# A mixed attention and expert kernel: normalisations by one two-scalar VectorE pass, the weight spreading on 128 rows, and the order set anew

## The reference

```python
def _layernorm(x, axis=-1, eps=1e-05):
    m = jnp.mean(x, axis=axis, keepdims=True)
    v = jnp.var(x, axis=axis, keepdims=True)
    return (x - m) / jnp.sqrt(v + eps)
...
x = x + _L0_xattn_ref(_layernorm(x, axis=-1), ctx_1024, ctx_1024, ...)
x = x + _L0_ffn_ref(_layernorm(x, axis=-1), ...)
x = x + _L1_xattn_ref(_layernorm(x, axis=-1), ctx_1024, ...)
x = x + _L1_ffn_ref(_layernorm(x, axis=-1), ...)
```

## Time and profile before

| | us |
|---|---|
| median of 3 runs | 326.61 |
| lowest, highest | 326.35, 327.21 |
| the profiled execution, its own time | 327.92 |
| its span in the trace | 325.9 |
| PE busy | 288.5 |
| DVE busy | 227.1 |
| ACT busy | 175.5 |
| POOL busy | 104.2 |

### The profile page before, as it was taken

How to read it: one execution, slowest core, us unless ns; L and a number is a source line. 1 busy time by engine, 2 the same in 40 slices (tenths; PEclk the granted TensorE clock), 3 DMA queues, 4 the chain that set the end, 5 groups by cost and what they waited for, 6 DMA issues and landing times.

```text
span 325.9 us, 7477 instructions
## 1 busy us (share of the span) xinstructions
PE 288.5 (89%) x2845; PEld 207.0 (64%) x2845; DVE 227.1 (70%) x641; ACT 175.5 (54%) x360; POOL 104.2 (32%) x109
## 2 busy tenths in 40 slices
PE   4598985887999978999999999776899999889994
PEld 4555663746566644565656676544666999569993
DVE  4769777898475389727478253879579996886533
ACT  3573743443478635483735867233963669535551
POOL 5930649393542011000001000112122666242631
PEclk9899998596999999999999999999999999999999
DMA  7700352423300000000000000000003120040121
GB/s 239 278 0 3 99 173 59 159 95 101 97 11 31 0 2 0 0 3 3 2 0 2 0 2 3 0 3 0 2 0 143 55 99 2 3 194 2 57 78 32
DMA packets 6634, 16.54 MB, mean 51 GB/s; under 512 B 708, under 2 KB 3016, under 8 KB 6600
## 3 DMA queue, kind: packets, MB, share of 16 engines
q1 hardware_dynamic: 6600, 16.08, 14.3%
HBM read 10.83 MB, written 0.52 MB: 35 GB/s over the span
## 4 chain that ended last, share of the span: by engine, by line
PE 65%; DVE 21%; POOL 5%; ACT 3%; issue 3%; DMA 1%; POOLq 0%; SPq 0%; DVEq 0%; ACTq 0%
PE ps L801 7%; PE ps L803 7%; PE ps L802 7%; PE ps L1037 6%; PE ps L984 4%; DVE MX L1405 3%; PE ps L955 3%; PE ps L953 3%; PE ps L956 2%; PE ps L874 2%; PE ps L862 2%; PE ps L1099 2%; PE ps L943 2%; PE ps L1129 2%; PE ps L863 2%
## 5 line engine op out<-in xcount | busy, mean ns | idle before, releaser
L1405 DVE TENSOR_REDUCE MX<-ps 128x8 f32<-128x512 f32 (+2 forms) x80 | 49.7, 680 | 13.4 <-PE ps L904 8.7
L1187 ACT ACTIVATE room<-ps 128x384 f32<-128x384 f32 (+1 forms) x96 | 46.2, 537 | 23.4 <-PE ps L956 15.3
L750 POOL TENSOR_SCALAR rstd<-mv 128x4 f32<-128x4 f32 x14 | 3.8, 272 | 134.1 <-DVE mv L1363 134.0
L773 POOL TENSOR_TENSOR wl<-wraw,wh 128x512 f16<-128x512 f32 (+1 forms) x30 | 35.6, 1215 | 31.7 <-DVE wh L1296 31.7
L664 POOL TENSOR_TENSOR room<-room 128x512 f16<-128x512 f32 x28 | 32.8, 1176 | 39.2 <-ACT room L1231 39.1
L812 PE MATMUL ps<-cst 128*128 128x128 f32 x142 | 25.0, 310 | 5.2 <-DMA cst<-in_const 4.2
L1037 PE MATMUL ps<-wd,room 128*128 128x128 f32 x144 | 23.3, 317 | 3.8 <-DVE room L1564 3.8
L812 PEld LDWEIGHTS ps<-cst 128*128 128x128 f32 x142 | 21.0, 216 | 8.2 <-DMA cst<-in_const 4.2
L1577 DVE TENSOR_TENSOR room<-ps,hr 128x512 f32<-128x512 f32 x28 | 19.1, 686 | 10.1 <-ACT hr L1225 8.8
L1037 PEld LDWEIGHTS ps<-wd,room 128*128 128x128 f32 x144 | 20.6, 222 | 6.5 <-DVE room L1564 4.4
L1231 ACT CAST room<-room 128x512 f16<-128x512 f32 x28 | 17.1, 618 | 11.7 <-DVE room L1577 11.5
(11 more groups left out here) (238 smaller groups left out, 836.7 us busy)
## 6 DMA issues: line engine op xcount, KB each, us to landing
wraw<-in_weights SPq DMA_DIRECT2D x8, 768.0 KB, 4.1
wraw<-wh SPq DMA_DIRECT2D x6, 384.0 KB, 2.9
wraw<-wl SPq DMA_DIRECT2D x6, 384.0 KB, 3.6
wraw<-in_weights SPq DMA_DIRECT2D x2, 576.0 KB, 7.3
rowb<-in_rows SPq DMA_DIRECT2D x1, 708.0 KB, 4.8
wd<-in_down SPq DMA_DIRECT2D x1, 576.0 KB, 7.4
X<-in_x SPq DMA_DIRECT2D x2, 256.0 KB, 4.4
picks<-in_spread SPq DMA_DIRECT2D x1, 512.0 KB, 5.7
```

The lines of the kernel that those rows point to most:

```text
L773: nc.gpsimd.tensor_tensor(wl[:, cols], wraw[:, i % 2, first:end], wh[:, cols], ALU.subtract).then_inc(w_ready, 1)
L1187: nc.scalar.activation(probabilities(a, b, u), src[:, 0:width], ACT.Exp, scale=SCALE[a]).then_inc(pr_ready, 1)
L1405: nc.vector.tensor_reduce(o, src[:].rearrange("p (h k) -> p h k", h=heads), AX_X, ALU.max).then_inc(max_read, 1)
```

## The change

- **Normalisations.** `ln_plain` is one piece on DVE: four `tensor_scalar` of 128 elements, one per token tile, (x - mean) * rstd with both as scalars per partition. DVE then waits for its own last one. `shift`, its semaphore and the ACT piece are gone.
- **Spreading.** `wpad` is 128 columns wide per tile instead of 64, so the transpose gives 128 rows; `wspread`, its copy and the matmul against `expsel` have 128 rows. The rows from 64 on are zero.
- **Rules.** In a pair of sequences the maxima of the second needn't come after the first's `negmax` any more; its `negmax` still does. The planner's cost of `ln_plain` is 1.0 on DVE.
- **Order.** `PRESSING` has other numbers, for 43 of the 49 entries of step.

```diff
-PRESSING = {..., 'ln_plain': 1411, 'ln_pow': 489, 'ln_stats': 1044, ...}
+PRESSING = {..., 'ln_plain': 1757, 'ln_pow': -1289, 'ln_stats': 1203, ...}
@@ attention()
-            before = [chain([("max", a, b, u) for u in range(12 if a == 1 else 4)] + [("negmax", a, b)], *before)]
+            before = [chain([("max", a, b, u) for u in range(12 if a == 1 else 4)], *before)]
+            chain([("negmax", a, b)], *before, *[("negmax", a, b - 1)] * (b % 2))
@@ parts()
     if k == "ln_plain":
-        return [("dve", .57), ("act", 1.65)]
+        return [("dve", 1.0)]
@@ build()
-        wpad = sb("wpad", [P, T, 64], F16)
+        wpad = sb("wpad", [P, T, P], F16)
...
-        wspread = [tF[0:64, g, 0:GT // 2].bitcast(F16) for g in range(G)]
+        wspread = [tF[:, g, 0:GT // 2].bitcast(F16) for g in range(G)]
...
-                        mm = nc.tensor.matmul(o[0:64, t * P:(t + 1) * P], wpad[:, t, :], identb[:], start=True, stop=True)
+                        mm = nc.tensor.matmul(o[:, t * P:(t + 1) * P], wpad[:, t, :], identb[:], start=True, stop=True)
...
-                        mm = nc.tensor.matmul(ps[bank[e][1]][:], expsel[0:64, x_:x_ + 1].broadcast_to([64, P]),
+                        mm = nc.tensor.matmul(ps[bank[e][1]][:], expsel[:, x_:x_ + 1].broadcast_to([P, P]),
                                               wspread[g], start=True, stop=True)
...
-                    nc.scalar.copy(wspread[e[1]], src[0:64, :]).then_inc(spread_ready, 1)
+                    nc.scalar.copy(wspread[e[1]], src[:]).then_inc(spread_ready, 1)
@@ ACT's queue
-                elif kind == "ln_plain":
-                    _, name, g = e
-                    from_, dst, _, _ = LN[name]
-                    k = nth[("ln_stats", name, g)] - 1
-                    sc.wait_ge(shift_ready, n)
-                    for t in range(T):
-                        ins = nc.scalar.activation(dst[:, g, t, :], from_[:, g, t, :], ACT.Identity, bias=shift[:, k, t:t + 1],
-                                                   scale=rstd[:, k, t:t + 1])
-                    ins.then_inc(plain_done, 1)
@@ DVE's queue
                 elif kind == "ln_plain":
-                    k = nth[("ln_stats",) + e[1:]] - 1
-                    dve.wait_ge(ln_rstd, nth[("ln_pow",) + e[1:]])
-                    for t in range(T):
-                        ins = nc.vector.tensor_scalar(shift[:, k, t:t + 1], mv[:, k, t, 0:1], rstd[:, k, t:t + 1], -1.0,
-                                                      ALU.mult, ALU.mult)
-                    ins.then_inc(shift_ready, 1)
+                    _, name, g = e
+                    from_, dst, _, _ = LN[name]
+                    k = nth[("ln_stats", name, g)] - 1
+                    dve.wait_ge(ln_rstd, nth[("ln_pow", name, g)])
+                    for t in range(T):
+                        ins = nc.vector.tensor_scalar(dst[:, g, t, :], from_[:, g, t, :], mv[:, k, t, 0:1], rstd[:, k, t:t + 1],
+                                                      ALU.subtract, ALU.mult)
+                    ins.then_inc(plain_done, 1)
+                    dve.wait_ge(plain_done, n)
```

More of the change, by code:

```diff
@@ L57 @@
 ARRIVES = {"ctx": 4.5, "masks0": 5., "masks1": 5., "bias": 7., ("split", 0): 5.5, "split": 14.0, ("ln_stats", "x0"): 7.0, "bo_add": 10.0, "kbs_zero": 8.5}
-PRESSING = {'add0': -408, 'add1': -1308, 'b3_add': -51, 'back': 744, 'bias': 929, 'bias_split': -399, 'bo_add': 1232, 'ctx': 951, 'down0': 576, 'down1': 359, 'downr': 1124, 'gate0': -1424, 'gate1': 1065, 'hi1': 1012, 'kblocks': -117, 'kbs_zero': -1339, 'ln_center': 83, 'ln_norm': 1593, 'ln_plain': 1411, 'ln_pow': 489, 'ln_stats': 1044, 'lo1': 1543, 'masks0': 320, 'masks1': 749, 'max': 334, 'nat': -86, 'negmax': 1829, 'o_take': -655, 'onehot': 426, 'onehot_t': -1823, 'out_norm': 1875, 'pv': -812, 'rank': 293, 'scores': -1610, 'sort_high': -1405, 'sort_low': 1667, 'spill': 245, 'split': 336, 'split_low': 436, 'spots': -1300, 'spread': 669, 'square': 1448, 'stack': -221, 'turn': 2557, 'up0': -841, 'up1': -41, 'v1': -1042, 'vctx': -868, 'xsplit': -353}
+PRESSING = {'add0': 63, 'add1': -1011, 'b3_add': 855, 'back': 391, 'bias': -267, 'bias_split': 1116, 'bo_add': 807, 'ctx': 1046, 'down0': -1303, 'down1': -1040, 'downr': 1177, 'gate0': -1424, 'gate1': 413, 'hi1': 1012, 'kblocks': -113, 'kbs_zero': -1339, 'ln_center': 367, 'ln_norm': 1835, 'ln_plain': 1757, 'ln_pow': -1289, 'ln_stats': 1203, 'lo1': -1154, 'masks0': -230, 'masks1': 760, 'max': 351, 'nat': -1025, 'negmax': 1917, 'o_take': -696, 'onehot': 936, 'onehot_t': -1823, 'out_norm': 1495, 'pv': -1096, 'rank': 818, 'scores': -1603, 'sort_high': -1404, 'sort_low': 1492, 'spill': 621, 'split': 336, 'split_low': 420, 'spots': -829, 'spread': 375, 'square': 871, 'stack': -221, 'turn': 2223, 'up0': 653, 'up1': -802, 'v1': -1399, 'vctx': -922, 'xsplit': -193}
 SHARED = 6
@@ L510, in build @@
         rstd = sb("rstd", [P, 7 * G, T])
-        shift = sb("shift", [P, 7 * G, T])
         lnx = sb("lnx", [P, G, T, P])
@@ L582, in build @@
         ln_stat, ln_rstd, ln_done = sem("ln_stat"), sem("ln_rstd"), sem("ln_done")
-        shift_ready, plain_done, b3_added = sem("shift_ready"), sem("plain_done"), sem("b3_added")
+        plain_done, b3_added = sem("plain_done"), sem("b3_added")
         centered = sem("centered")
```

## The result

The changed kernel took 336.99 us (median of 4 runs, 336.91 to 338.15) where the kernel before took 326.91 beside it: ratio 1.0329, 95% interval 1.0301 to 1.0357. The prediction was 324.3, with 330.5 as the top of its range. The profiled execution has a span of 335.0 us (325.9 before): PE busy 286.5 us (2.0 less), DVE 245.3 (18.2 more), ACT 164.0 (11.5 less), POOL 104.5 (as before). So PE was busy 2 us less and idle 11 us longer.

The account below looks back on a forecast made before the run. The prediction took PE to bound the kernel (65% of the last chain, DVE 21%). Its terms, 4.5 + 0.8 - 3.0 - 2.4 - 1.0 - 1.2 = -2.3, gave 324.3 us from a 326.61 median; 8-in-10 range 314 to 330.5.

Parts of the forecast that it names:

- The new order, "gives some 0.5 back": Start: both transposes first and attention 0's score maxima in a row were to return some 0.5 us.
- Start, +4.5: x0 at the start: group 1's pass held once per POOL addition or memset, delaying what follows; 4.5 us lost.
- x1 to the gates, +0.8: x1 to layer 0's gates: residues hold three of four passes per group, the second gate speeds up; net 0.8 us lost.
- The clock there, -3.0: Behind layer 0's second gate: PE stays busy, so the half-clock stretch goes; 3.0 us gained.
- Spreading, -2.4: Experts: with 128 rows, twelve spreading matmuls without a PE gap each save 0.2 us; 2.4 us gained.
- x2, -1.0: Handoff from layer 0, group 1: the unheld pass and steps covering PE's wait gain 1.0 us.
- x3 of group 0, -1.2: Third normalisation of group 0: PE waits there and POOL is free, so the shorter pass gains 1.2 us.
- x3 of group 1, 0: Third normalisation of group 1: 1.3 us saved, one or two holds paid; net 0, bounds -1 and +2.
- The third: Rival: all four instructions held at x0 group 1, x1 twice and x3 group 1; 329.5 us, chance 0.22.
- Rivals 1, 2 and 4: Memsets don't hold the pass: 318.9, chance 0.20; two-scalar form never held: 313.1, chance 0.13; spreading does nothing: 326.7, chance 0.05.

Follow-up runs that it names:

- e14: e7 with the order of the kernel before on PE, DVE and ACT up to the end of attention 0: 325.7 us.
- e7: e4 with x1 of both groups in the old form (shifts on DVE, normalisation on ACT): 328.4 us.
- e4: The changed kernel with POOL's two additions and its memsets made to wait for both passes of x0: 332.2 us.
- e2: The kernel before with the 128-row spreading alone, the shift written over the mean to make room: 324.9 us.
- e8: e2 with the pass on DVE only for x2 of both groups and x3 of group 0: 325.7 us.
- e11: e7 with attention 0's own steps on PE, DVE and ACT in the order of the kernel before, at the same queue places: 329.7 us.
- e13: The changed kernel with the order of the kernel before up to the end of attention 0, and x0 and x1 by shift and ACT: 323.9 us.
- e12: e11 with x3 of group 1 in the old form too (shift on DVE, normalisation on ACT): 329.1 us.
- e3: The changed kernel's order with the old normalisation (shifts on DVE, rest on ACT) and the 64-row spreading: 335.6 us.
- e15: The changed kernel with its order only from attention 0's end to mid attention 1, before's elsewhere; x0, x1 and x3 of group 1 by ACT: 322.5 us.
- e1: The kernel before, with its own order and 64-row spreading, and only the normalisation pass moved to DVE: 338.9 us.
- e10: e1 with POOL's additions and memsets made to wait for both passes of x0: 333.0 us.
- e6: The changed kernel with the same bytes zeroed by sixteen smaller memsets instead of three: 338.6 us.
- e9a: The changed kernel with POOL waiting for its own memset behind each of the two kbs memsets: 336.8 us.
- e9b: The changed kernel with a wait on an already satisfied semaphore in front of each of the three big memsets: 337.1 us.
- e5: The changed kernel with only POOL's memsets waiting for both passes of x0, the two additions left in place: 334.2 us.

## Why the prediction was wrong

The forecast was -2.3 us and the traces differ by +9.2 at the last product. Of the 11.5 between them, 5.8 stand in the start and attention 0 (+10.3 against +4.5), 4.4 between the second gate and layer 1's experts (-3.2 against -7.6), 2.0 in the last stage (+2.0 against 0), and x1 gives back 0.8 (0.0 against +0.8).

**The new order, "gives some 0.5 back": the step that failed most.** Attention 0 was priced in half a sentence inside the start's +4.5, from the fact that the maxima stand in a row. They do, and PE has too little beside them: +3.8 us from the first maximum to the end of attention 0, 1.9 with full clock and 1.9 from the half clock at 34 to 42 us. e14 gives 2.7 us for that order once nothing is held.

**Start, +4.5: right in kind, wrong in its rule and short by what follows.** It had each DVE instruction wait for one POOL instruction, "because the memsets use the same instruction stream as the additions". Additions and residues do that (1.17 to 1.24 us each). The second and third pass instead stayed until the row of memsets was over, so the pass ended at 19.9, not 17.7. That rule cost the forecast little: it had the bias split held by the last memset anyway, and `nat q0` came at 21.7, near its 21.0. What followed cost more than the 0.8 us allowed: with half clock to 24.7 us the first maximum came at +6.5, 1.7 more than `nat q0`.

**x1 to the gates, +0.8: right.** The holds are as drawn, three of four. From the end of group 0's attention 0 to the second gate's weights both kernels take 28.8 us: 2.85 lost ahead of the gate, 2.8 gained in it. The hold costs 3.8 us all the same (e7 against e4), because the faster gate doesn't need the held pass: e7 has it too.

**The clock there, -3.0: mostly not cashed.** The half clock behind the gate is gone in the changed kernel. Over 50 to 85 us before lost 8.5 us of full speed, the changed kernel in 60 to 95 only 3.4. But PE now rests instead (0.29 us of work in 84 to 86): half clock had stood where PE would have waited for DVE. From the gate to the first product of layer 1, where clock, spreading and both handoffs were to give 7.6 us, it gained 3.2. If the spreading gives its 2.2 here (e2) and the handoffs nothing (e8), some 1.0 is left for the clock; no run takes it by itself.

**Spreading, -2.4: right**, -2.2 in e2. **x2, -1.0, and x3 of group 0, -1.2: nothing came** (e8, in before's order). The wait of 1.69 us at the handoff is one of several that end together. **x3 of group 1, 0: +2.0 in the last stage**, at its upper bound. In the new order that stage took 82.3 us with the pass (changed, e7, e11, e13 and e14), and with the old form 81.7 in e12 but 82.7 in e3; in before's order 80.3 with the old form (e2, e8, e15) and 81.6 with the pass (e1, e10). So the order costs at least 1.4 there, and the pass 1.3 in before's order, held as at x1. What it costs in the new order isn't shown: e12 and e3 point opposite ways.

**Rivals.** The third, slower by full holds, had the right side with 329.5; its mechanism, all four instructions held, appears nowhere. Rivals 1, 2 and 4 are refuted by the 6.73 us, by x1 and by e2.

What isn't explained: why the clock falls in attention 0 in the changed kernel and e6, and not in e9a and e9b with the same order. The 2 us that e9a and e9b gain there are gone by the first product of layer 1: in both the clock is at half for some 3 us between 106 and 110.5, where the changed kernel has 1.00.

## What to carry to other kernels

Before work is moved to VectorE, ask what GpSimd does at that moment and what stands behind the instruction in VectorE's queue: one instruction of the pass took 0.34 us alone, 1.2 beside an addition, 6.7 beside an addition and a row of memsets. The queue behind it decided what that was worth: freeing the pass brought the first maximum 4.3 us forward in the new order (e4) and 6.4 in the old (e10). Saved latency at a wait is only worth what no other wait takes over; three places at 1.2 us gave nothing. And a new order should be tried in pieces: this one lost 2.7 us in front (by medians) and some 1.4 at the end, and gained 3.7 in the middle (by traces).

## What the runs showed of the hardware

- A row of GpSimd memsets can hold a VectorE `tensor_scalar` from SBUF to SBUF for longer than one of them: 6.73 us over the second addition and three memsets (6.62 in e1 and e9b), 7.27 over an addition and sixteen small ones, at most 2.93 with own waits between. It does not always: in e5 one was let in after the first of three memsets (1.98 us). What decides is not shown. The Trainium skill, "SBUF — State Buffer", section "Who interferes with whom", has the shared ports held for one whole instruction. The trace agrees for additions and residues (1.17 to 1.24 us) and for that instruction of e5, and not for the held passes.
- A `scalar_tensor_tensor` on 256 elements, all in SBUF, is held by an addition (1.37 us before, L1283) and not by a memset: 0.49 us in e5, from 17.07 on, inside a memset from 16.83 to 18.78.
- The two-scalar pass on f32 isn't faster than one with two tensors: 341 ns against 343, and 136 ns above the one-element shift's 205, about 1 ns per element. The Trainium skill, "VectorE: DVE Perf Modes", section "The perf-mode tier table", lists `tensor_scalar` on f32 at twice the plain speed; for this form, at 128 elements, no run here shows it. One-scalar forms that read f32 and write 16 bits took 0.22 us for 128 elements (L1266) and 0.35 for 256 (L1273); no run here tells whether the second scalar or the f32 output makes the difference.
- The norms with two tensors (L1386) are held too: four took 2.94 us at 269.96 beside POOL's residues of the hidden values, where one takes 0.34 us unheld (median). Maxima and products that read PSUM never were: all 80 maxima lie between 656 and 692 ns, and the 16 products of layer 0 between 673 and 690.
- A weight load of 64 rows isn't loaded ahead as one of 128 is. Before, the load of L1025 started at 84.78, 0.30 us after the matmul in front of it and with its own (84.79); now it starts with the matmul in front (90.34), 0.22 us ahead of its own. That was worth 2.2 us for 16 of them (e2). PE's loads, before and then now:

```profile
84.78 0.09 PEld L1025 LDWEIGHTS ps<-tF,expsel 64*128 64x128 bf16 x1 [0.42 <-issue]
```
```profile
90.34 0.10 PEld L1025 LDWEIGHTS ps<-tF,expsel 128*128 128x128 bf16 x1
```
